# A new order of the calls on all five engines, with the first eight filler matmuls kept and the other 24 taken out

## The chip, the cores and the metric

The kernel runs on one core of one Trainium2 chip. The core has five engines that run side by side, each with its own instruction stream in a fixed order: PE (TensorE, matmuls and transposes), DVE (VectorE), ACT (ScalarE), POOL (GpSimd) and SP (SyncE, here only a queue that issues transfers). They meet at semaphores: an instruction waits until a counter has reached a number, and everything behind it on its engine waits with it. The metric is the device time of one execution in microseconds (us). Three timed executions of the kernel before gave 276.61 us in the median (275.88 to 279.37).

## The reference, cut to what matters

The input is 8 batches of 1024 tokens with 128 features, all float32. One transformer layer is applied to it:

```
q = rope(x @ wq) / sqrt(128);  k = rope(x @ wk) / sqrt(128);  v = x @ wv
p = softmax(causal(q @ k.T))                       # one head, 1024 x 1024 per batch
x1 = layernorm(x + (p @ v) @ wo)
h  = gelu(x1 @ bw1.T + b1)                         # bw = mean|w| * sign(w), 128 -> 512
out = layernorm(x1 + h @ bw2.T + b2)               # 512 -> 128
```

The rotary part turns only the first 64 of the 128 features of q and k; the other 64 are copied.

## The kernel before, in words

A batch (index `c`, 0 to 7; in the code `B - 1` is 7) has 1024 tokens: eight tiles of 128 tokens (index `r` or `t`) in two halves of four (index `h`). Each step of the work is a small function of the engine that does it, and at the end of each engine's block stands a list of calls, written out by hand, some hundreds of lines long. That list is the order. Batches overlap: while the scores of batch `c` are made, the feed-forward part of batch `c - 2` or `c - 3` runs.

The steps of one batch, as they feed one another:

- SP `stripes(c)` (L222): four transfers bring x of batch `c` into `xq`, in pieces of 32 tokens by 32 features. They wait until both halves of the batch before have been turned (`s_xT`), because `xq` is one buffer. For batch 1 the four transfers are not in a call: they stand at L214, third in SP's queue. Their landing counts up `s_xq_in`.
- DVE `x_squares(h, c)` (L1580): transposes `xq` into `xT`. Half 0 waits for all four transfers of its batch. Batch 0 goes another way: `turn_x0` on PE.
- ACT `xT_high`, then POOL `xT_low` (for batch 0 DVE `x0T_low`): split xT in a rounded part and a rest, so that fast matmuls on both parts give float32 accuracy.
- PE `project(h, c)`: q and k of a half. DVE `rotate(h, c)` (L1598): three multiplications with the cosine and sine tables, which ACT's queue loads at the start (L991, L992). ACT `tok_copy`: the features that aren't turned. POOL `rotation_sum` adds the products (for batch 0 DVE `first_rotation_sum`, L1586).
- PE `turn_qk(n, c)`: transposes q (n = 0, 2) and k (n = 1, 3) of a half. ACT `qkT_high` and DVE `qkT_low` (L1617) split them.
- PE `scores(r, c)` into a two-bank tile of PSUM, DVE `row_max`, ACT `exponentials`, DVE `turn_row` (32 by 32 squares). SP `carry(g, c)` (L233): 16 transfers that move the squares between partitions into `probT`; group 0 is rows 0 to 3, group 1 rows 4 to 7. For rows 4 to 7 of batches 0 and 7 PE's `turn_row` with `row_copy` on ACT and DVE takes the place of this.
- PE `weigh_group` or `weigh_row`, ACT `pxT_copy`, PE `project_out`, DVE `residual1`, `statistics1`, POOL `first_factors`, DVE `first_norm`: attention output and first layer norm. `wvo`, the product of wv and wo, is made once by `setup_turn_wv` and `setup_wvo`.
- PE `turn_x1`, ACT `x1T_high`, DVE `x1T_low`, PE `up`, ACT `gelu` and `hidden_high`, POOL `hidden_low`, PE `down`, ACT `y_half`, PE `turn_y`, DVE `residual2`, `statistics2`, POOL `second_factors`, ACT (some POOL) `second_norm`, SP `store`: feed-forward part and second layer norm. Its weights are set up once by ACT `setup_signs`, PE `setup_turn_sgn1` and `setup_turn_sgn2`, ACT `setup_magnitudes` and `setup_weights`.

PSUM has three two-bank tiles (`pairs`) and two single banks (`banks`), handed out in the order of PE's calls. A call that takes one waits until the reader of its last user is done (`wait_freed`, L493).

Two helpers on PE compute nothing: `keep_warm(n)` (L486) and `fill(n)` (L557) multiply a tile of zeros. They are the fillers: `keep_warm` 8 at the very start, then 4, 3 and 6, `fill` 2 in the first batch, 7 and 2 near the end, 32 in all.

Of the kernel before, what the change touches and what calls it, by code (L numbers as in the profile page):

```python
# [16 lines left out]
def attention_ffn_kernel(nc, x, wq, wk, wv, wo, w1, b1, w2, b2, cos_t, sin_t, out):  # L17
# [10 lines left out]
    B, T, D = x.shape  # L28
# [27 lines left out]
    with ctx:  # L56
# [88 lines left out]
        def sems(name, n):  # L145
# [5 lines left out]
            sems("s_qk", NG), sems("s_qkT", 4), sems("s_score", NT), sems("s_px", NT), sems("s_attn", NG))  # L151
# [52 lines left out]
        def _(sp):  # L204
# [28 lines left out]
            def carry(g, c):  # L233
# [4 lines left out]
                if c > 0:  # L238
                    sp.wait_ge(s_px[GROUPS[g][-1]], c)
# [32 lines left out]
            carry(1, 3)  # L272
            stripes(B - 1)
            carry(0, B - 4)
# [3 lines left out]
            carry(0, B - 3)  # L278
            tokens(B - 2)
            store(0)  # L280
            carry(1, B - 3)
            carry(0, B - 2)
            store(1)
# [14 lines left out]
        def _(pool):  # L298
# [96 lines left out]
            xT_low(1, 1)  # L395
            rotation_sum(0, 1)
            rotation_sum(1, 1)
            xT_low(0, 2)
# [3 lines left out]
            xT_low(1, 3)  # L402
            first_factors(0, 0)
            rotation_sum(1, 2)
            rotation_sum(0, 3)
            first_factors(1, 0)
            xT_low(0, B - 4)
            xT_low(1, B - 4)
            rotation_sum(1, 3)
            first_factors(0, 1)  # L410
            first_factors(1, 1)
            rotation_sum(0, B - 4)
            rotation_sum(1, B - 4)
# [3 lines left out]
            xT_low(0, B - 3)  # L417
            hidden_low(3, 0)
            first_factors(0, 2)
            xT_low(1, B - 3)  # L420
            first_factors(1, 2)
            rotation_sum(0, B - 3)
# [5 lines left out]
            first_factors(0, 3)  # L428
            second_factors(0)
            rotation_sum(1, B - 3)  # L430
            first_factors(1, 3)
            xT_low(1, B - 2)
            hidden_low(0, 2)
            rotation_sum(0, B - 2)
            hidden_low(1, 2)
            hidden_low(2, 2)
            hidden_low(3, 2)
            rotation_sum(1, B - 2)
            xT_low(0, B - 1)
# [3 lines left out]
            xT_low(1, B - 1)  # L443
            rotation_sum(0, B - 1)
            hidden_low(0, 3)
            hidden_low(1, 3)
            hidden_low(2, 3)
            hidden_low(3, 3)
            second_factors(2)
            first_factors(0, B - 3)  # L450
            rotation_sum(1, B - 1)
# [3 lines left out]
            hidden_low(2, B - 4)  # L455
            hidden_low(3, B - 4)
            second_factors(3)
# [27 lines left out]
        def _(pe):  # L485
# [71 lines left out]
            def fill(n):  # L557

                wait_freed(*list(pair_of)[-len(pairs)])
                for _ in range(n):  # L560
                    pe.matmul(pairs[len(pair_of) % len(pairs)][:, 0:BANK], warm[:, 0:P], warm[:, :], start=True, stop=True)
# [1569 lines left out]
```

## Time and profile before

| What | Value |
|---|---|
| Timed executions, median of 3 | 276.61 us (275.88 to 279.37) |
| Profiled execution, span from first to last instruction | 274.5 us |
| What lies around the span, against the median | 2.1 us |
| PE busy | 260.9 us, 95% of the span |
| DVE, ACT, POOL busy | 229.6 (84%), 224.7 (82%), 167.2 us (61%) |
| Mean granted TensorE clock | 0.993 of full speed |

The span is that of one profiled execution; no time of its own stands beside it, so it is set against the median. A busy share counts an engine's instructions from start to modelled end, so PE at 95% can still have some slack between the starts of its matmuls. A row of a timeline gives the start, the duration, the engine, the line and what is written and read; in square brackets stands how long the engine was idle before it and who ended that. Waits of SP's queue aren't marked: they show as gaps between its issues.

### The profile page before, as it was taken

What the parts mean: (1) busy time and instruction counts of PE and PEld (TensorE: products, weight loads), DVE (VectorE), ACT (ScalarE), POOL (GpSimd) and SP (SyncE); (2) the same over time, 40 slices, a digit from 0 to 9 for tenths busy, and PEclk for the clock granted to TensorE, in tenths of its full rate; (3) what the DMA queues carried; (4) which work ended last, traced back from release to release, by engine and by line L of the source; (5) the groups of instructions that cost most, each with busy time, mean ns of one, the idle gap of its engine ahead of it and who ended that gap; (6) DMA issues with size and microseconds to landing.
All of it is one profiled execution on the core that took longest, in us unless ns stands there. A gap on an engine that the chain in (4) does not pass through costs nothing.

```text
span 274.5 us, 5184 instructions
## 1 busy us (share of the span) xinstructions
PE 260.9 (95%) x1485; PEld 208.7 (76%) x1487; DVE 229.6 (84%) x638; ACT 224.7 (82%) x398; POOL 167.2 (61%) x258
## 2 busy tenths in 40 slices
PE   7899999999999999999999999999999999999960
PEld 3678989987779588868879688868886878897630
DVE  2799999999999996999979987998689738537984
ACT  3378964565897989996998999898999799999972
POOL 3033132613625698399821998497819887887772
PEclk9999999999999999999999999999999999999997
DMA  7944596479657936833685318825830720200323
GB/s 178 166 61 87 107 145 98 115 163 192 104 132 160 199 94 153 180 47 78 173 187 127 82 39 249 184 71 151 189 73 27 197 55 2 76 2 0 111 90 108
DMA packets 58012, 31.94 MB, mean 116 GB/s; under 512 B 33408, under 2 KB 54400, under 8 KB 57984
## 3 DMA queue, kind: packets, MB, share of 16 engines
q1 hardware_dynamic: 57024, 30.76, 50.4%
q10 hardware_dynamic: 960, 0.85, 1.3%
q8 instruction: 12, 0.20, 0.3%
q14 instruction: 16, 0.13, 0.2%
HBM read 9.18 MB, written 4.19 MB: 49 GB/s over the span
## 4 chain that ended last, share of the span: by engine, by line
PE 81%; DVE 6%; ACT 5%; issue 3%; DMA 2%; ACTq 1%; POOL 0%; POOLq 0%
PE pair L589 18%; PE bank L606 18%; PE bank L632 5%; PE bank L674 4%; PE pair L650 4%; PE pair L651 4%; PE bank L620 4%; PE bank L682 4%; PE bank L683 4%; PE bank L719 2%; DMA sin_sb<-in_sin_dram 2%; PE pair L663 2%; PE pair L665 2%; PE pair L664 2%; PE bank L639 2%
## 5 line engine op out<-in xcount | busy, mean ns | idle before, releaser
L391 POOL TENSOR_TENSOR hid_lo<-hid,hid_hi 128x1024 fp32r<-128x1024 f32 x28 | 66.0, 2386 | 19.7 <-ACT hid_hi L1075 19.7
L1004 ACT ACTIVATE prob<-pair,negmax 128x128 f32<-128x128 f32 (+3 forms) x64 | 47.2, 742 | 14.2 <-DVE negmax L1457 12.5
L606 PE MATMUL bank<-probT,xa 128*128 128x512 f32 (+3 forms) x160 | 54.2, 482 | 0.0
L1457 DVE CUSTOM_DVE_ANT_0 pair<-pair,mask_row 128x128 f32<-128x128 f32 (+3 forms) x64 | 47.9, 759 | 6.1 <-PE pair L589 5.5
L606 PEld LDWEIGHTS bank<-probT,xa 128*128 128x128 f32 x160 | 29.1, 190 | 20.2 <-issue 15.3
L341 POOL TENSOR_TENSOR xT_lo<-xT,xT_hi 128x512 fp32r<-128x512 f32 x14 | 18.0, 1288 | 40.4 <-ACT xT_hi L1034 40.4
L1467 DVE STREAM_TRANSPOSE turned<-prob 128x128 f32<-128x128 f32 (+7 forms) x56 | 39.5, 724 | 0.5 <-ACT prob L1004 0.5
L589 PE MATMUL pair<-qkT_hi 128*128 128x512 f32 (+3 forms) x96 | 36.0, 375 | 0.8 <-DVE qkT_lo L1619 0.3
L1068 ACT ACTIVATE hid<-pair,b_sb,alpha 128x1024 f32<-128x1024 f32 x28 | 32.9, 1209 | 0.1
L589 PE MATMUL pair<-qkT_lo,qkT_hi 128*128 128x512 f32 (+3 forms) x96 | 32.8, 342 | 0.0
L589 PE MATMUL pair<-qkT_hi,qkT_lo 128*128 128x512 f32 (+3 forms) x96 | 32.8, 342 | 0.0
L1075 ACT ACTIVATE hid_hi<-hid 128x1024 fp32r<-128x1024 f32 x28 | 28.6, 1057 | 0.0
L335 POOL TENSOR_TENSOR ln<-ln,minus_half 128x4 f32<-128x4 f32 (+1 forms) x21 | 26.2, 1249 | 1.6
L1102 ACT ACTIVATE res<-res,ln 128x128 f32<-128x128 f32 x52 | 23.1, 496 | 3.6 <-POOL ln L377 3.6
L1056 ACT ACTIVATE qkT_hi<-bank 128x512 fp32r<-128x512 f32 x32 | 18.5, 598 | 7.3 <-PE bank L674 7.2
L1619 DVE TENSOR_TENSOR qkT_lo<-bank,qkT_hi 128x512 fp32r<-128x512 f32 x32 | 21.1, 680 | 3.4 <-ACT qkT_hi L1056 3.4
L349 POOL TENSOR_TENSOR tok<-rot_cos,rot_sin 128x512 f32<-128x512 f32 x14 | 18.0, 1288 | 9.4 <-DVE rot_sin L1614 9.4
L650 PE MATMUL pair<-x1T_hi,sgn1T 128*128 128x512 f32 x56 | 23.4, 418 | 0.3 <-issue 0.3
L682 PE MATMUL bank<-hid_hi,sgn2T 128*128 128x512 f32 x56 | 22.3, 399 | 0.0
L683 PE MATMUL bank<-hid_lo,sgn2T 128*128 128x512 f32 x56 | 22.2, 396 | 0.0
L651 PE MATMUL pair<-x1T_lo,sgn1T 128*128 128x512 f32 x56 | 22.1, 395 | 0.0
L1567 DVE TENSOR_TENSOR res<-bank,x 128x512 f32<-128x512 f32 x16 | 10.9, 687 | 12.5 <-PE bank L719 12.4
(116 smaller groups left out, 649.9 us busy)
## 6 DMA issues: line engine op xcount, KB each, us to landing
probT<-turned SPq DMA_DIRECT2D x96, 116.0 KB, 2.3
probT<-turned SPq DMA_DIRECT2D x128, 52.0 KB, 2.0
xq<-in_L_attn_x_dram SPq DMA_DIRECT2D x28, 128.0 KB, 4.0
xa<-in_L_attn_x_dram SPq DMA_DIRECT2D x7, 512.0 KB, 4.7
out_dram<-res SPq DMA_DIRECT2D x7, 512.0 KB, 3.3
hid<-in_L_ffn_w_dram SPq DMA_DIRECT2D x2, 256.0 KB, 3.2
out_dram<-res SPq DMA_DIRECT2D x2, 256.0 KB, 2.3
xa<-in_L_attn_x_dram SPq DMA_DIRECT2D x1, 256.0 KB, 3.6
```

The costliest lines, as they stand in the source:

```text
L391: pool.tensor_tensor(hid_lo[:, j, :], hid[:, j, :], hid_hi[:, j, :].bitcast(F32), ALU.subtract).then_inc(s_hid_lo[j], 1)
L589: ins = pe.matmul(dst[:, lo:hi], qp[:, 0, me], kp[:, 1, lo - first:hi - first], start=n == 0, stop=n == 2)
L606: ins = pe.matmul(bank_of["px", g, c][:, 0:n * P], xa[c % 2][:, j, :], probT[g][:, :, TG * j:TG * j + n, :].rearrange("p n m i -> p m n i" ...
L650: pe.matmul(dst[:, half(h)], sgn1T[:, j, :], x1T_hi[:, half(h)], start=True, stop=False)
L651: ins = pe.matmul(dst[:, half(h)], sgn1T[:, j, :], x1T_lo[:, half(h)], start=False, stop=True)
L682: pe.matmul(dst[:, :], sgn2T[:, j, :], hid_hi[:, j, half(h)], start=j == 0, stop=False)
L683: ins = pe.matmul(dst[:, :], sgn2T[:, j, :], hid_lo[:, j, half(h)], start=False, stop=j == NF - 1)
L1004: act.activation(prob[r % 3][:, 0:(r + 1) * P], pair_of["score", r, c][:, slice(*columns(r))], ACT.Exp, scale=-1.0, bias=negmax[:, r:r + 1 ...
L1068: act.activation(hid[:, j, :], pair_of["up", j, c][:, :], ACT.Gelu, bias=b1_sb[:, j:j + 1], scale=alpha1[:, j:j + 1]).then_inc(s_gelu[j], 1)
L1075: act.activation(hid_hi[:, j, :], hid[:, j, :], ACT.Copy).then_inc(s_hid_hi[j], 1)
L1457: dve.tensor_tensor_reduce(mine, mine, mask_row[:, T - (r + 1) * P:T], -1.0, -MASKED, ALU.add, ALU.min, negmax[:, r:r + 1]).then_inc(s_max ...
L1467: dve.transpose(turned[g][:, :, squares(r, 0, r), :].rearrange("p k m j -> p m k j"), prob[r % 3][:, 0:(r + 1) * P].rearrange("p (m k j) - ...
```

## The change

It keeps every call but the fillers, and puts the lists of all five engines in another order. Of the fillers only `keep_warm(8)` stays; `fill` and its definition go. The semaphore `s_px` has one counter for each group of rows in place of one for each row; the waits on it mean what they meant. The diff has some 1,600 lines; these are the parts that matter at the start, in SP's queue and at the end.

```diff
@@ SP
             stripes(3)
+            stripes(B - 4)
             tokens(1)
-            stripes(B - 4)
             carry(0, 1)
             carry(1, 1)
+            stripes(B - 3)
             tokens(2)
-            stripes(B - 3)
...
@@ PE, start
             turn_x0(0)
             turn_x0(1)
-            keep_warm(4)
             project(0, 0)
             project(1, 0)
-            keep_warm(3)
             turn_qk(0, 0)
             turn_qk(1, 0)
-            keep_warm(6)
             setup_turn_wv()
             scores(0, 0)
+            setup_wvo()
             scores(1, 0)
-            fill(2)
-            turn_qk(2, 0)
             scores(2, 0)
             scores(3, 0)
-            setup_wvo()
+            turn_qk(2, 0)
+            turn_qk(3, 0)
             project(0, 1)
-            turn_qk(3, 0)
             project(1, 1)
+            scores(4, 0)
             setup_turn_sgn1()
             setup_turn_sgn2()
-            scores(4, 0)
...
             project(0, 3)
             project_out(1, 0)
+            weigh_group(0, 0, 3, 1)
+            turn_qk(2, 2)
             scores(0, 2)
             scores(1, 2)
-            weigh_group(0, 0, 3, 1)
-            turn_qk(2, 2)
...
@@ PE, end
             down(1, B - 2)
             turn_x1(1, B - 1)
-            fill(7)
             turn_y(0, B - 2)
             turn_y(1, B - 2)
-            fill(2)
             up_half(1, 0, B - 1)
...
@@ ACT, start
             xT_high(0, 0)
             xT_high(1, 0)
+            xT_high(0, 1)
             tok_copy(0, 0)
             qkT_high(0, 0)
             qkT_high(1, 0)
             tok_copy(1, 0)
-            xT_high(0, 1)
+            exponentials(0, 0)
+            xT_high(1, 1)
+            exponentials(1, 0)
+            exponentials(2, 0)
+            qkT_high(2, 0)
+            exponentials(3, 0)
+            qkT_high(3, 0)
             setup_signs()
-            exponentials(0, 0)
-            exponentials(1, 0)
-            xT_high(1, 1)
-            exponentials(2, 0)
-            exponentials(3, 0)
-            qkT_high(2, 0)
-            qkT_high(3, 0)
             setup_magnitudes()
             tok_copy(0, 1)
+            xT_high(0, 2)
             tok_copy(1, 1)
...
@@ DVE, start
             setup_wqk()
             x0T_low(0)
             x0T_low(1)
+            x_squares(0, 1)
+            x_squares(1, 1)
             rotate(0, 0)
             first_rotation_sum(0)
             rotate(1, 0)
-            x_squares(0, 1)
             qkT_low(0, 0)
             qkT_low(1, 0)
+            setup_wvT()
             first_rotation_sum(1)
-            setup_wvT()
             row_max(0, 0)
+            x_squares(0, 2)
             row_max(1, 0)
-            x_squares(1, 1)
+            row_max(2, 0)
             turn_row(0, 0)
-            row_max(2, 0)
+            setup_wvo()
             row_max(3, 0)
-            setup_wvo()
...
             row_max(4, 0)
+            x_squares(1, 2)
             row_max(5, 0)
...
             row_max(1, 1)
-            qkT_low(2, 1)
-            qkT_low(3, 1)
-            rotate(0, 2)
-            row_max(2, 1)
-            turn_row(0, 1)
-            turn_row(1, 1)
             x_squares(0, 3)
             x_squares(1, 3)
+            qkT_low(3, 1)
+            row_max(2, 1)
             row_max(3, 1)
+            turn_row(1, 1)
```

From batch 1 on the lists are shuffled throughout, mostly by one to three places on PE and by up to some ten on DVE and ACT; no call changes its engine, its size or its waits.

## Rows read from the trace of the kernel before

**Rows 1.** Stretches: us, busy (instructions) of PE, PEld, DVE, ACT, POOL, granted clock, DMA, GB/s.
```profile
27.26:32.32 5.06, 4.96 (x43) 4.44 (x42) 4.86 (x11) 5.06 (x13) 0.76 (x1) 1.00 0.31 78
32.40:246.40 214.00, 213.04 (x1216) 173.32 (x1215) 184.07 (x511) 183.07 (x310) 140.83 (x209) 1.00 0.54 122
...
267.10:270.70 3.60, 0.00 (x0) 0.00 (x0) 2.69 (x13) 0.88 (x2) 2.22 (x4) 1.00 0.34 103
270.90:274.40 3.50, 0.00 (x0) 0.00 (x0) 0.53 (x2) 0.80 (x2) 0.00 (x0) 0.50 0.48 149
```
**Rows 2.** PE's waits: who it waited for, us in total, times, longest.
```profile
PE bank L719 <- ACT yT L1093: 1.2, 2, 1.0
```
**Rows 3.** Chain of waits, first 40 us: start us, us, what.
```profile
2.21 6.63 DMA sin_sb<-in_sin_dram
8.87 0.69 DVE rot_cos L1611
...
12.21 0.62 DVE xT L1584
...
13.93 1.78 DVE tok L1589
...
22.57 0.61 ACT tok L1041
```
**Rows 4.** The four transfers of x of batch 1: durations, starts; issue to landing.
```profile
L214 SPq DMA_DIRECT2D xq<-in_L_attn_x_dram x4: 443/1484/3146, 1.8 to 6.1; - x4
...
DMA to landing us min/median/max: 5.4/7.1/7.9
```
**Rows 5.** Timelines of DVE, POOL and ACT: start us, us, what [idle before <- ended by].
```profile
10.26 0.69 DVE L1589 TENSOR_TENSOR tok<-rot_cos,rot_sin 128x512 f32<-128x512 f32 x1
...
13.87 1.29 POOL L341 TENSOR_TENSOR xT_lo<-xT,xT_hi 128x512 fp32r<-128x512 f32 x1 [10.23 <-ACT xT_hi L1034]
...
13.66 0.64 ACT L1009 ACTIVATE hid<-hid 128x512 f32<-128x512 f32 x1
...
28.78 1.12 ACT L1004 ACTIVATE prob<-pair,negmax 128x1024 f32<-128x1024 f32 x1
```
**Rows 6.** Timeline of PE in the first 16 us.
```profile
9.62 0.82 PE L489 MATMUL pair<-warm 128*128 128x512 bf16 x3
11.00 1.09 PE L674 MATMUL bank<-ident,tok 128*128 128x128 f32 x8 [0.56 <-DVE tok L1589]
...
14.15 0.30 PE L589 MATMUL pair<-qkT_hi 128*128 128x128 f32 x1 [0.29 <-DVE qkT_lo L1619]
```
**Rows 7.** Timeline of PE from 27.26 us: first and last of five rows, all transposes.
```profile
27.26 0.60 PE L674 MATMUL bank<-ident,tok 128*128 128x128 f32 x4
...
31.96 0.60 PE L674 MATMUL bank<-ident,tok 128*128 128x128 f32 x4
```
**Rows 8.** Timeline of SP's queue: start us, us, transfers issued.
```profile
31.11 2.70 SPq L226 DMA_DIRECT2D xq<-in_L_attn_x_dram  x4
...
38.52 2.32 SPq L226 DMA_DIRECT2D xq<-in_L_attn_x_dram  x4
40.94 22.25 SPq L242 DMA_DIRECT2D probT<-turned  x32
```
**Rows 9.** The page, issues of transfers: KB each, median us from issue to landing.
```profile
probT<-turned SPq DMA_DIRECT2D x128, 52.0 KB, 2.0
xq<-in_L_attn_x_dram SPq DMA_DIRECT2D x28, 128.0 KB, 4.0
```
**Rows 10.** Timelines of PE and ACT: one row at 54 us, then near the end.
```profile
54.58 2.32 PE L606 MATMUL bank<-probT,xa 128*128 128x512 f32 x8
...
254.89 1.46 PE L561 MATMUL pair<-warm 128*128 128x512 bf16 x6
...
257.30 0.59 PE L561 MATMUL pair<-warm 128*128 128x512 bf16 x2
...
255.47 0.78 ACT L1093 ACTIVATE yT<-bank,b_sb,alpha 128x512 f32<-128x512 f32 x1
```

More of the change, by code:

```diff
@@ L609, in weigh_group @@
                 if last == rows[-1]:
-                    ins.then_inc(s_px[last], 1)
+                    ins.then_inc(s_px[g], 1)
             def weigh_row(r, c):
@@ L755, in _ @@
             turn_row(7, 0)
-            turn_qk(3, 1)
+            project(0, 2)
             scores(0, 1)
             scores(1, 1)
-            project(0, 2)
+            weigh_group(0, 0, 3, 0)
+            turn_qk(3, 1)
             scores(2, 1)
-            weigh_group(0, 0, 3, 0)
             scores(3, 1)
+            project_out(0, 0)
             scores(4, 1)
+            turn_qk(0, 2)
             scores(5, 1)
-            project_out(0, 0)
             scores(6, 1)
-            turn_qk(0, 2)
             scores(7, 1)
@@ L839, in _ @@
             scores(4, B - 4)
+            turn_y(1, 0)
             project_out(0, 3)
-            weigh_group(1, 0, 3, 3)
             scores(5, B - 4)
             scores(6, B - 4)
+            weigh_group(1, 0, 3, 3)
             weigh_group(1, 4, 7, 3)
@@ L901, in _ @@
             scores(7, B - 2)
+            weigh_group(1, 0, 3, B - 3)
+            weigh_group(1, 4, 7, B - 3)
             turn_x1(1, B - 4)
-            weigh_group(1, 0, 3, B - 3)
+            project(1, B - 1)
             turn_qk(0, B - 1)
-            weigh_group(1, 4, 7, B - 3)
+            turn_qk(1, B - 1)
             up(0, B - 4)
             up(1, B - 4)
-            turn_qk(1, B - 1)
-            project(1, B - 1)
             project_out(1, B - 3)
@@ L915, in _ @@
             up(3, B - 4)
+            turn_y(1, 3)
+            turn_qk(2, B - 1)
             scores(0, B - 1)
-            turn_y(1, 3)
+            scores(1, B - 1)
             weigh_group(0, 0, 3, B - 2)
-            scores(1, B - 1)
-            turn_qk(2, B - 1)
+            turn_qk(3, B - 1)
             scores(2, B - 1)
-            turn_qk(3, B - 1)
             scores(3, B - 1)
@@ L961, in _ @@
             weigh_row(7, B - 1)
+            up(3, B - 2)
+            turn_y(1, B - 3)
             turn_x1(0, B - 1)
@@ L1149, in _ @@
             qkT_high(2, 1)
[L1150 removed]
             exponentials(0, 1)
[L1152 to L1153 removed]
             tok_copy(0, 2)
             pxT_copy(0, 0)
+            qkT_high(3, 1)
+            exponentials(1, 1)
+            xT_high(0, 3)
             exponentials(2, 1)
@@ L1171, in _ @@
             qkT_high(2, 2)
+            exponentials(0, 2)
             qkT_high(3, 2)
@@ L1208, in _ @@
             xT_high(1, B - 3)
-            x1T_high(1, 1)
-            exponentials(5, 3)
             exponentials(6, 3)
             pxT_copy(1, 2)
+            x1T_high(1, 1)
+            tok_copy(1, B - 4)
             qkT_high(0, B - 4)
@@ L1734, in _ @@
             first_norm(7, 0)
-            statistics1(0, 1)
+            residual1(0, 1)
+            residual1(1, 1)
+            residual1(2, 1)
+            residual1(3, 1)
+            x1T_low(0, 0)
+            turn_row(3, 2)
             turn_row(4, 2)
+            x1T_low(1, 0)
+            row_max(6, 2)
+            reciprocals(0, 2)
             row_max(7, 2)
-            x1T_low(1, 0)
+            rotate(1, 3)
+            qkT_low(0, 3)
             turn_row(5, 2)
             turn_row(6, 2)
-            reciprocals(0, 2)
-            statistics1(1, 1)
-            statistics1(2, 1)
-            statistics1(3, 1)
             turn_row(7, 2)
@@ L1850, in _ @@
             x1T_low(1, 2)
+            rotate(0, B - 2)
             residual1(4, 3)
@@ L1913, in _ @@
             residual1(7, B - 4)
-            statistics2(1, 1)
+            rotate(0, B - 1)
+            qkT_low(2, B - 2)
             statistics1(4, B - 4)
```

736 lines of the change are left out of this document (359 added, 377 removed).

## The prediction

> **What bounds the kernel now.** I read the stretches first. From 32.4 to 246.4 us PE is busy for 213.04 of 214.00 us at the full granted clock [rows 1]: in the middle PE is the bound, and a new order can win at most the 1.0 us of idle time there (a little more if slack hides between the starts of its matmuls). The middle is nearly eight tenths of the span, so what the order can change for the better lies mostly before and behind it. Whatever PE loses at the start it doesn't get back, since it has no idle time in which to catch up.
>
> Next, the chain of waits of the first 40 us. The start isn't PE's. The sine table lands after 2.21 + 6.63 = 8.84 us, DVE begins the first rotation at 8.87, and from there the chain runs along DVE almost without a break to 22.57 [rows 3]; only then does it pass to PE. So a microsecond that DVE loses before 22.57 is one that the whole kernel loses. Two pieces on this chain matter below: the transpose of x of batch 1 (12.21, 0.62 us) and the second rotation sum (13.93, 1.78 us).
>
> Then the queue. The four transfers of x of batch 1 were issued between 1.8 and 6.1 us, and none landed in under 5.4 us [rows 4]. The last one therefore landed at 6.1 + 5.4 = 11.5 us or later. In the kernel before nobody notices, because the transpose that needs them starts only at 12.2.
>
> **The change part by part.** *The first transposes.* In the new list of DVE x_squares(0, 1) and x_squares(1, 1) stand ahead of rotate(0, 0). The first waits for all four transfers, and DVE takes its calls strictly in turn. So DVE stands still until 11.5, transposes twice (2 x 0.62 [rows 3]) and starts the first rotation at about 12.8 instead of 8.87: **+3.9 us**. Queued behind are the rotation sum, both copies of ACT, and turn_qk on PE; everything of batch 0 waits for those. Nothing else in the change touches these transfers: the queues of SP and ACT keep their first calls as they are.
>
> Part of it comes back. The transpose at 12.21 is no longer between rotation and scores: **-0.6** (x_squares(0, 2) comes in later, in the place of the second transpose). The second rotation sum took 1.78 us beside a subtraction of POOL (13.87, 1.29 us), the first one 0.69 with POOL idle [rows 3, 5]. In the new order that subtraction follows the transpose at about 13 and is over before either sum: **-1.1**.
>
> Part is added. ACT's two sign activations ran before at 13.66, when ACT had nothing else to do; a pair of them takes about 1.1 us [rows 5]. They and xT_high(0, 2), another 0.6, now stand ahead of tok_copy(1, 1). I follow ACT from the shifted rotation on: most of it is hidden behind DVE's work for the same rows, some 0.5 us shows, and 0.2 us more where DVE waits for ACT's first copy of q: **+0.7**. So the exponentials of row 7, batch 0, at 28.78 before [rows 5], move by 3.9 - 0.6 - 1.1 + 0.7 = **+2.9**, and the transposes of rows 6 and 7 on PE with them. Bounds of this: +2.2 if ACT's added work is hidden whole, +4.3 if POOL's subtraction still collides and the waits stand (3.9 - 0.6 + 0.7, and 0.3).
>
> *A second landing of the same kind.* x_squares(0, 3) now stands right behind row_max(1, 1), ahead of qkT_low(3, 1) and row_max(2, 1). Its transfers are issued in 2.7 us from 31.11 before [rows 8], now some 3.4 us later because carry(0, 0) is; with 4.0 us to land [rows 9] they are there at about 40.5. I count DVE there at about 38. Behind it wait scores(4, 1) and the exponentials of rows 2 and 3; PE has other calls for most of that time. **+0.4**, bounds 0 and the whole 2.5.
>
> *The fillers at the start.* keep_warm(4), (3), (6) and fill(2) all stand in front of work that waits for something else (turn_qk for the rotation sum, scores for qkT_low [rows 6]); taking them out gives **0**. What they cover is the clock. With them gone PE is idle from about 9.9 until turn_qk(0, 0), which moves from 11.00 to about 15.0: 5.1 us. At the end of the trace the granted clock was still 1.00 at 270.7, 3.6 us after PE's last instruction, and 0.50 (1.2 GHz) from 270.9 [rows 1]. 5.1 is longer than 3.6, so I expect the clock to fall before PE starts again. The calls that then run at half speed on the chain: turn_qk(0, 0) takes 0.44 more, scores(0, 0) 0.36 more (it takes 0.36 from 14.15 to the next call), turn_qk(2, 0) and (3, 0) 0.4 more each: **+1.6**. Bounds: 0, if the clock stays, and +3, if both project(_, 1) (2 x 1.5 us) run at half speed too and DVE has no slack for it.
>
> The Trainium skill has a rule that bears on this stretch (TensorE: Matmul & The Clock Gate, section Part 4: PE-mode transpose): transposes on PE don't count as busy for the clock. This case's trace doesn't show it: from 27.26 to 32.32 PE did nothing but 43 transposes and the clock stayed at 1.00 [rows 1, 7], whereas 3.6 us without any instruction ended in its fall. By the rule the two turn_qk at 15 us would not help the clock back up; that is a rival below.
>
> *The fillers near the end.* fill(7) runs until 254.89 + 1.46 = 256.35, but turn_y waits for ACT's yT, which ends at 255.47 + 0.78 = 256.25 [rows 10]: 0. fill(2) takes 0.59 at most [rows 10] of which half is pipeline: **-0.3**. The gaps there stay under 2 us, so the clock should hold.
>
> *The rest.* On PE most calls move by one to three places. That the middle has 1.0 us to win and no bound below for what a bad neighbour can cost makes me take **0**, with -1 and +3 as ends. s_px is a renaming: 0.
>
> **Sum.** 2.9 + 0.4 + 1.6 - 0.3 = +4.6 us on the span of 274.5: 279.1. Around the span lie 2.1 us against the median of 276.61 (276.61 - 274.5), so 281.2 us, or 1.7% over it. A measurement tells about 2% from no change here: 271.1 and 282.1 us are the borders.
>
> **The rivals.**
>
> *A, the sum above:* 281.2; with its own terms between 279.5 and 283.
>
> *B, the clock holds.* The 5.1 us gap might straddle what the clock looks at, or turn_qk may come in time. 281.2 - 1.6 = 279.6. For it: one fall in the whole trace is thin evidence. Against it: the gap is longer than the one after which it fell.
>
> *C, SP's queue becomes the bound: slower.* carry(0, 1) starts at 40.94, right behind stripes(4), which waited until 38.52 for x_squares(1, 3); two carries take 22.25 us to issue, one half of that [rows 8]. So the last transfer of carry(0, 1) is issued near 52.1 and lands 2.0 us later [rows 9], at 54.1, while weigh_group(0, 0, 3, 1) takes it at 54.58 [rows 10]: 0.5 us to spare. In the new order tokens(1) (0.6) moves in between, x_squares(1, 3) waits for the later landing above, and weigh_group(0, 0, 3, 1) comes two calls (0.8) earlier. If the queue shifts by more than PE does, PE waits in this batch and, as the queue issues without a break for batch after batch, in the next ones. It decides from about half a microsecond of extra shift; once there, the price is the queue's shift of 3.5 on top: 284.7.
>
> *D, the start is won back: no slower.* If the clock holds, the second landing is hidden, and the new order removes the 1.0 us of idle time in the middle [rows 1] and the 1.2 us for yT at the end [rows 2]: 274.5 + 2.9 - 0.3 - 1.0 - 1.2 + 2.1 = 277.0. It needs everything to go well at once in the rows that a new order can reach.
>
> *E, transposes don't count for the clock (the rule of the Trainium skill above).* It falls and comes back only in the course of project(0, 1) and (1, 1): half of the 3.0 us more that those two take at half speed shows, +1.5 over A: 282.7. Rows 7 speak against it.
>
> **How the numbers follow.** A 0.45, B 0.24, C 0.17, D 0.10, E 0.04. The predicted time is A's, 281.2 us. D at its low side and the upper half of C stay out of the range: 277.0 to 284.7. A lies within 2% in three cases of four, so slower by over 2%: 0.11 (A) + 0.17 (C) + 0.03 (E) = 0.31. Faster by over 2% would need 5.5 us, more than all idle time that rows 1 and 2 leave: 0.03. Within 2%: 0.66.
>
> **What would show it.** Right: in DVE's timeline an idle time of some 4 us ahead of the first transpose, ended by the transfer of xq; rot_cos first at about 12.8; PE idle from 9.9 to about 15; a granted clock of 0.5 somewhere between 13 and 25 us; the middle still PE's, shifted as a whole by 4 to 5 us. Wrong: rot_cos near 9 (then the landing isn't as late as I read it), a clock of 1.00 throughout (B), new waits of PE for probT between 50 and 120 us (C), or a chain of waits that leaves PE in the middle.

## The result: 301.06 us, and where the time went

The kernel after takes 301.06 us (median; 300.6 to 301.33) against 276.55 of the kernel before (four executions of each): a ratio of 1.0877, 95% interval [1.0822, 1.0932]. The profiled execution has a span of 299.2 us and took 301.02. I had predicted 281.2 with 284.7 as the upper end; the loss is 24.5 us, five times the 4.6 of my sum.

PE's waits of after, the five largest of the whole span (us in total, times, longest us; in before the largest was the 1.2 us of [rows 2]):

```profile
PE bank L633 <- DVE x L1487: 9.3, 5, 3.8
PE bank L668 <- DVE tok L1577: 4.4, 1, 4.4
PE bank L633 <- DVE res L1473: 2.8, 1, 2.8
PE bank L713 <- ACT yT L1081: 2.7, 2, 1.6
PE bank L668 <- DVE x1T_lo L1548: 2.6, 2, 1.6
```

One row of these was predicted: the 4.4 us for tok is the start. The largest wasn't. Line 633 is turn_x1, which transposes the first norm's output, and L1487 is first_norm on VectorE (line 1499 of before). In the middle, where PE had 1.0 us of idle time in 214 [rows 1], PE now waits for VectorE. The same in stretches of after, for PE alone (stretch, us, PE busy, granted clock, DMA share, GB/s):

```profile
13.50:23.70 10.20, 8.11 (x32) 0.50 0.40 53
23.80:90.00 66.20, 66.03 (x431) 1.00 0.60 125
90.00:231.00 141.00, 129.22 (x682) 1.00 0.50 115
231.95:235.37 3.42, 3.42 (x12) 0.50 1.02 275
235.40:252.40 17.00, 12.88 (x67) 1.00 0.15 38
252.43:255.85 3.42, 3.42 (x16) 0.50 0.02 5
```

Up to 90 us the middle is full, as before. From 90 to 231 us PE is idle for 11.8 us, and the clock falls to 0.50 (1.2 GHz) in two more stretches of 3.42 us. Each begins about 1 us after a stop of PE, the one of 2.76 us (it ends at 230.96) and the other of 3.76 (at 251.38). A step that both kernels have shows the same without any grouping; the start of scores(7, c) on PE, after minus before, in us:

```
batch c      0     1     2     3     4     5     6      7    last call of PE
shift     +4.9  +4.8  +4.3  +6.3  +8.1  +9.8  +14.0  +17.3   +24.7
```

So 4.9 us are lost in batch 0, nothing in the next two, 13.0 in the five batches behind them and another 7.4 behind the last scores, 20.4 in all.

What VectorE does there is in the view of one line (duration ns min/median/max, first and last start, forms). first_norm of after:

```profile
L1487 DVE TENSOR_SCALAR x<-res,ln x64: 306/341/2427, 61.3 to 278.2; 128x128 f32<-128x128 f32 x64
L1473 DVE SCALAR_TENSOR_TENSOR res<-bank,rinv,xa x64: 305/340/351, 46.2 to 274.7; 128x128 f32<-128x128 f32 x64
```

The same line in before:

```profile
L1499 DVE TENSOR_SCALAR x<-res,ln x64: 306/342/436, 56.2 to 253.1; 128x128 f32<-128x128 f32 x64
```

The median has not changed; 19 of the 64 are over 0.4 us now, and the group's busy time is 42.8 us instead of 18.7. Its neighbour residual1 (L1473), of the same size, is as fast as ever. What a long one stands beside is seen in the timeline of after between 94 and 104 us, VectorE first (start, us, operation; "x2" are two in a row):

```profile
94.14 0.34 DVE L1487 TENSOR_SCALAR x<-res,ln 128x128 f32<-128x128 f32 x1
94.40 1.12 DVE L1473 SCALAR_TENSOR_TENSOR res<-bank,rinv,xa 128x128 f32<-128x128 f32 x4
95.44 0.68 DVE L1599 TENSOR_TENSOR rot_cos<-pair,cos_sb 128x512 f32<-128x512 f32 x1
96.69 1.48 DVE L1487 TENSOR_SCALAR x<-res,ln 128x128 f32<-128x128 f32 x1
98.10 1.09 DVE L1445 CUSTOM_DVE_ANT_0 pair<-pair,mask_row 128x896 f32<-128x896 f32 x1
99.11 3.68 DVE L1487 TENSOR_SCALAR x<-res,ln 128x128 f32<-128x128 f32 x2
102.71 1.43 DVE L1455 STREAM_TRANSPOSE turned<-prob 128x512 f32<-128x512 f32 x2
```

and POOL and PE in the same stretch:

```profile
95.73 6.98 POOL L391 TENSOR_TENSOR hid_lo<-hid,hid_hi 128x1024 fp32r<-128x1024 f32 x3 [2.91 <-ACT hid_hi L1063]
102.85 0.66 PE L633 MATMUL bank<-ident,x 128*128 128x128 f32 x4 [2.00 <-DVE x L1487]
```

first_norm(4, 1) at 94.14 takes 0.34 us with POOL idle. From 95.73 POOL runs three hidden_low in a row, each about 2.3 us. The next first_norm takes 1.48 and ends at 98.17, just when the first hidden_low is over; the two at 99.11 end at 102.79, just behind the third. In between row_max (98.10) runs at its own speed beside the second hidden_low, and the transposes behind 102.71 do beside POOL's next instruction. PE waits 2.00 us for the last first_norm. In before all four calls stood ahead of rotate(1, 4) and row_max(6, 3). The last two of them, and the first hidden_low, in before:

```profile
89.69 0.60 DVE L1499 TENSOR_SCALAR x<-res,ln 128x128 f32<-128x128 f32 x2
93.12 7.04 POOL L391 TENSOR_TENSOR hid_lo<-hid,hid_hi 128x1024 fp32r<-128x1024 f32 x3
```

They were through at 90.3, and POOL began at 93.1. The new order puts the last three of the four behind rotate(1, 4), two of them behind row_max(6, 3) too, and so into POOL's stretch. Such meetings occur in batches 2 to 7 as well. Of the 19 long first_norm, 16 end just behind a hidden_low and 3 just behind POOL's xT_low, a subtraction of 128x512 that takes 1.29 us.

Not every POOL instruction has this effect. Two first_norm of batch 3 beside a small one of POOL, in after:

```profile
151.49 0.59 DVE L1487 TENSOR_SCALAR x<-res,ln 128x128 f32<-128x128 f32 x2
151.45 1.04 POOL L335 TENSOR_TENSOR ln<-ln,minus_half 128x4 f32<-128x4 f32 x1
```

They took their usual time and were done 0.4 us ahead of POOL. All 20 first_norm that began beside one of POOL's small instructions (128x4 to 128x16) took less than 0.4 us.

The start went as predicted. VectorE and PE of after:

```profile
11.21 1.30 DVE L1572 STREAM_TRANSPOSE xT<-xq 128x512 f32<-128x512 f32 x2 [3.34 <-DMA xq<-in_L_attn_x_dram]
12.44 0.65 DVE L1599 TENSOR_TENSOR rot_cos<-pair,cos_sb 128x512 f32<-128x512 f32 x1
14.54 1.97 PE L668 MATMUL bank<-ident,tok 128*128 128x128 f32 x8 [4.41 <-DVE tok L1577]
```

Against [rows 3] the rotation begins at 12.44 instead of 8.87, behind two transposes that wait for xq.

The chain of waits of after passes to VectorE accordingly, by engine and by line (page):

```profile
PE 63%; DVE 24%; issue 5%; DMA 2%; ACT 2%; POOL 1%; SPq 1%; ACTq 0%; POOLq 0%; DVEq 0%
PE pair L583 13%; DVE x L1487 9%; PE bank L600 7%; PE bank L668 5%; PE bank L676 4%; PE bank L677 4%; PE bank L626 4%; PE pair L644 4%; PE pair L645 4%; PE bank L614 4%; DVE pair L1445 4%; DVE turned L1455 3%; PE pair L685 2%; DVE stat L1564 2%; DMA xq<-in_L_attn_x_dram 2%
```

### The profile page after: what moved, and what is told of

Its sections match the earlier page's. It is cut to its first block, busy times and chain, and to the rows that moved or that the text cites. A ratio compares the mean times of both kernels' runs of the same rounds, so it can differ in the third digit from the quotient of the medians.

```text
span 299.2 us, 5138 instructions
## 1 busy us (share of the span) xinstructions
PE 264.5 (88%) x1463; PEld 213.4 (71%) x1463; DVE 253.2 (85%) x638; ACT 225.4 (75%) x398; POOL 167.9 (56%) x258
## 4 chain that ended last, share of the span: by engine, by line
PE 63%; DVE 24%; issue 5%; DMA 2%; ACT 2%; POOL 1%; SPq 1%; ACTq 0%; POOLq 0%; DVEq 0%
PE pair L583 13%; DVE x L1487 9%; PE bank L600 7%; PE bank L668 5%; PE bank L676 4%; PE bank L677 4%; PE bank L626 4%; PE pair L644 4%; PE pair L645 4%; PE bank L614 4%; DVE pair L1445 4%; DVE turned L1455 3%; PE pair L685 2%; DVE stat L1564 2%; DMA xq<-in_L_attn_x_dram 2%
## 5 line engine op out<-in xcount | busy, mean ns | idle before, releaser
L391 POOL TENSOR_TENSOR hid_lo<-hid,hid_hi 128x1024 fp32r<-128x1024 f32 x28 | 65.9, 2376 | 22.4 <-ACT hid_hi L1063 22.2
L992 ACT ACTIVATE prob<-pair,negmax 128x128 f32<-128x128 f32 (+3 forms) x64 | 47.3, 741 | 25.6 <-DVE negmax L1445 20.4
L600 PE MATMUL bank<-probT,xa 128*128 128x512 f32 (+3 forms) x160 | 53.6, 483 | 0.6 <-DMA probT<-turned 0.3
L600 PEld LDWEIGHTS bank<-probT,xa 128*128 128x128 f32 x160 | 29.5, 190 | 24.2 <-issue 18.7
L1487 DVE TENSOR_SCALAR x<-res,ln 128x128 f32<-128x128 f32 x64 | 42.8, 713 | 1.5 <-POOL ln L369 0.9
L1455 DVE STREAM_TRANSPOSE turned<-prob 128x128 f32<-128x128 f32 (+7 forms) x56 | 38.7, 715 | 1.6 <-ACT prob L992 1.5
L583 PE MATMUL pair<-qkT_lo,qkT_hi 128*128 128x512 f32 (+3 forms) x96 | 34.0, 354 | 0.0
L583 PE MATMUL pair<-qkT_hi,qkT_lo 128*128 128x512 f32 (+3 forms) x96 | 34.0, 354 | 0.0
L668 PE MATMUL bank<-ident,tok 128*128 128x128 f32 x128 | 20.0, 292 | 7.3 <-DVE tok L1577 4.4
L323 POOL TENSOR_TENSOR ln<-stat 128x4 f32<-128x4 f32 (+1 forms) x21 | 4.4, 210 | 37.3 <-DVE stat L1478 28.9
L1090 ACT ACTIVATE res<-res,ln 128x128 f32<-128x128 f32 x52 | 22.3, 492 | 3.8 <-POOL ln L377 3.6
L668 PEld LDWEIGHTS bank<-ident,tok 128*128 128x128 f32 x128 | 16.1, 152 | 9.7 <-issue 4.7
```

Source lines behind the costliest of these rows:

```text
L391: pool.tensor_tensor(hid_lo[:, j, :], hid[:, j, :], hid_hi[:, j, :].bitcast(F32), ALU.subtract).then_inc(s_hid_lo[j], 1)
L583: ins = pe.matmul(dst[:, lo:hi], qp[:, 0, me], kp[:, 1, lo - first:hi - first], start=n == 0, stop=n == 2)
L600: ins = pe.matmul(bank_of["px", g, c][:, 0:n * P], xa[c % 2][:, j, :], probT[g][:, :, TG * j:TG * j + n, :].rearrange("p n m i -> p m n i" ...
L668: ins = pe.transpose(dst[:, t * P:(t + 1) * P], tok[:, TG * (n // 2) + t, (n % 2) * D:(n % 2 + 1) * D], ident[:, :])
L992: act.activation(prob[r % 3][:, 0:(r + 1) * P], pair_of["score", r, c][:, slice(*columns(r))], ACT.Exp, scale=-1.0, bias=negmax[:, r:r + 1 ...
L1455: dve.transpose(turned[g][:, :, squares(r, 0, r), :].rearrange("p k m j -> p m k j"), prob[r % 3][:, 0:(r + 1) * P].rearrange("p (m k j) - ...
```

## The experiments

Where an edit adds lines to the kernel, the lines behind it move by two or three in the rows: first_norm is then L1489, L1490 or L1501 and hidden_low L393.

Theory L: a first_norm that is due while a POOL instruction runs stands still until that instruction ends, and this is where the middle goes. (By the rows above, "a POOL instruction" has to be read as one of its large subtractions.) Theory O: the order's other waits hold the middle, and the long first_norm is a by-product. Theory P, for one run: it is POOL's length, hid_lo being late, that costs.

### Taking POOL's long instruction away, with a control

```diff
 def hidden_low(j, c):
+    if c == 0: pool.memset(hid_lo[:, j, P:T].bitcast(F32), 0.0)
-    pool.tensor_tensor(hid_lo[:, j, :], hid[:, j, :], hid_hi[:, j, :].bitcast(F32), ...)
+    pool.tensor_tensor(hid_lo[:, j, 0:P], hid[:, j, 0:P], hid_hi[:, j, 0:P].bitcast(F32), ...)
```

The rest of hid_lo is set to zero once, so seven eighths of this correction are left out.

> The changed kernel with POOL's hidden_low cut from 1024 to 128 columns (the other columns of hid_lo are set to zero once, so the low part of the hidden layer is left out there). Theory L (a DVE first_norm that starts while a POOL instruction is running stands still until that one ends): the 19 first_norm that took up to 2.43 us in the changed kernel fall to about 0.34, DVE's total for them from 42.8 to some 22 us, PE's waits for them (9.3 us) go, and the time falls by about 19 us to 280 to 284 us; what stays is the start's 4.8 us. Theory O (the place of first_norm in DVE's list is what PE waits for, whatever POOL does): first_norm may get shorter but PE's waits ahead of turn_x1 stay, 296 to 301 us.

> The control: the same cut of POOL's hidden_low in the kernel before. There only one first_norm of 64 was longer than 0.4 us, so by theory L, and by theory O, nothing is won: 274 to 278 us. If this one falls by 5 us or more as well, POOL's work itself was a bound, and the cut in the changed kernel proves nothing of the meeting of DVE and POOL.

Measured: 280.21 us in the order of after (1.0125 times before, [1.0076, 1.0173]) and 276.63 in the order of before (0.9999, [0.9979, 1.002]). The groups of a_small_lo (busy us, mean ns, idle before):

```profile
L1489 DVE TENSOR_SCALAR x<-res,ln 128x128 f32<-128x128 f32 x64 | 20.6, 367 | 1.8 <-POOL ln L369 1.2 <-POOL ln L335 0.6
L393 POOL TENSOR_TENSOR hid_lo<-hid,hid_hi 128x128 fp32r<-128x128 f32 x28 | 13.0, 466 | 33.7 <-ACT hid_hi L1065 33.6
```

and first_norm of the control:

```profile
L1501 DVE TENSOR_SCALAR x<-res,ln 128x128 f32<-128x128 f32 x64 | 18.6, 338 | 0.6 <-POOL ln L369 0.3
```

The order of before doesn't care how long hidden_low is; the order of after gets 20.9 us back, and PE's wait for x is gone. What is left over the control, 3.6 us, is the start: PE's scores(7, c) is 5.2 us late in batch 0 and between 4.3 and 5.1 in all others, and its last call 3.9. Part of the 20.9 us comes by way of the clock: without the stops it stays at 1.00 from 23.3 us to the end of PE's work, and the two stretches of 3.42 us at half speed are gone, by estimate 1.7 us each.

### Making POOL wait instead

```diff
 def hidden_low(j, c):
+    if j == 0:
+        pool.wait_ge(s_x1[1] if c < 5 else s_x1[0], c + 2)
     pool.wait_ge(s_hid_hi[j], c + 1)
```

> The changed kernel, whole computation, with one wait more on POOL: hidden_low(0, c) starts only when the first_norm of the half that met it (second half of batch c+1, for c = 5 and 6 first half of batch c+2) is done. No call changes its place. Theory L: the long first_norm go (all but a few under 0.4 us), POOL's hidden_low move back by 2 to 4 us, which its idle time of 44% takes; 281 to 288 us. Theory O: a wait more can only cost, 300 to 306 us.

For c = 5 and 6 the edit waits for the first half of batch c + 1, not c + 2 as written there. Measured: 305.37 us (1.1043, [1.0993, 1.1093]): a miss for L's number, and inside O's 300 to 306. The groups of a_yield, and then four of PE's waits:

```profile
L393 POOL TENSOR_TENSOR hid_lo<-hid,hid_hi 128x1024 fp32r<-128x1024 f32 x28 | 65.9, 2375 | 51.0 <-DVE x L1489 46.6 <-ACT hid_hi L1065 4.4
L1489 DVE TENSOR_SCALAR x<-res,ln 128x128 f32<-128x128 f32 x64 | 25.3, 441 | 5.0 <-POOL ln L335 4.2 <-POOL ln L369 0.9
```

```profile
PE bank L678 <- POOL hid_lo L393: 6.6, 5, 2.0
PE bank L715 <- ACT yT L1083: 5.1, 3, 2.4
PE bank L635 <- DVE x L1489: 5.0, 1, 5.0
PE bank L602 <- DVE qkT_lo L1609: 2.5, 1, 2.5
```

first_norm did get short (25.3 us), and PE's project(0, 6), at 133.5 us, comes 5.0 earlier than in after. But POOL now stands idle for 46.6 us until first_norm is through, with all that follows in its list late too: PE waits 6.6 us for POOL's hid_lo, a wait that after does not have, and scores(5, 5), at 159.2 us, is already 1.8 later than in after. The clock is at 0.50 for 17.1 us behind 150 us, against 6.8 in after. So the run adds a wait of its own and can't decide between L and O by its time. I had left out the price of that wait: POOL's list had no room for it.

### Cutting hidden_low into four

```diff
-    pool.tensor_tensor(hid_lo[:, j, :], hid[:, j, :], hid_hi[:, j, :].bitcast(F32),
-                       ALU.subtract).then_inc(s_hid_lo[j], 1)
+    for q in range(4):
+        part = slice(q * T // 4, (q + 1) * T // 4)
+        ins = pool.tensor_tensor(hid_lo[:, j, part], hid[:, j, part], hid_hi[:, j, part].bitcast(F32),
+                                 ALU.subtract)
+    ins.then_inc(s_hid_lo[j], 1)
```

> The kernel after, where each hidden_low (POOL, 128x1024) is issued as four instructions of 256 columns; the result is the same and its total POOL time grows: from the 128x128 form's 0.46 us and the 128x1024 form's 2.37 us a piece is some 0.73 us, so four are 2.93, and 28 of them cost POOL 15 us more. Theory L (VectorE's first_norm stands still while a POOL instruction runs, and a stop ends with the POOL instruction): the longest first_norm falls from 2.43 us to about 1.1, the excess of all 64 over their 0.34 from 24 us to 8 to 14, and the time from 301 to 287 to 293. Theory P (it is POOL's own length, or hid_lo being late, that costs, and cutting hidden_low short removed that): 301 to 312. Theory O (the order's other waits): 299 to 303.

Measured: 286.95 us (1.0358, [1.0303, 1.0413]), 14.1 less than after, with all work done. The groups of a_split4:

```profile
L393 POOL TENSOR_TENSOR hid_lo<-hid,hid_hi 128x256 fp32r<-128x256 f32 x112 | 78.1, 731 | 17.0 <-ACT hid_hi L1066 16.9
L1490 DVE TENSOR_SCALAR x<-res,ln 128x128 f32<-128x128 f32 x64 | 29.3, 502 | 1.5 <-POOL ln L369 0.9 <-POOL ln L335 0.6
```

POOL works 12 us longer and the kernel is 14 us faster, so P falls. The longest first_norm is 892 ns now, the length of a piece (731) plus a part of its own: of the 27 over 0.4 us, 26 end just behind a piece and one behind xT_low. O had 299 to 303; L had 287 to 293, and the time lies at its lower end.

### Only the order, the instructions untouched

```diff
 first_norm(4, 1)
+first_norm(5, 1); first_norm(6, 1); first_norm(7, 1)    # from behind rotate(1, 4), row_max(6, 3)
 ...
+residual2(1, 0); first_norm(4..7, 2)                    # ahead of turn_row(2, 4)
 ...
 first_norm(4, 3)
+first_norm(5..7, 3)                                     # from behind turn_row(3, 5)
 ...
 first_norm(4, 5)
+first_norm(5..7, 5)                                     # from behind turn_row(3, 7)
```

> The kernel after with thirteen calls of VectorE's list put earlier and nothing else: first_norm(5..7,1), (5..7,3) and (5..7,5) directly behind first_norm(4,.) of their batch, and residual2(1,0) with first_norm(4..7,2) ahead of turn_row(2,4), so that these groups are done when POOL's next hidden_low begins. In the trace of after these 13 calls carry 15.3 of the 24 us by which first_norm is longer than 0.34 each. Theory L (it is only that first_norm meets hidden_low): first_norm's excess falls to 8 to 11 us, and the time from 301 to 285 to 291. Theory O (the new order's other waits hold the middle; the same instructions in a slightly other order change nothing): 298 to 303.

Measured: 288.11 us (1.0417, [1.0356, 1.0478]), 12.9 less than after: thirteen first_norm and one residual2 put earlier in one engine's list give back half of the loss. VectorE of a_early where the rows above were taken:

```profile
94.45 1.10 DVE L1487 TENSOR_SCALAR x<-res,ln 128x128 f32<-128x128 f32 x4
95.47 1.12 DVE L1473 SCALAR_TENSOR_TENSOR res<-bank,rinv,xa 128x128 f32<-128x128 f32 x4
```

and POOL:

```profile
96.04 7.05 POOL L391 TENSOR_TENSOR hid_lo<-hid,hid_hi 128x1024 fp32r<-128x1024 f32 x3 [2.91 <-ACT hid_hi L1063]
```

Four first_norm in 1.10 us, over before POOL begins at 96.04. The group's busy time falls from 42.8 to 28.0; eight long ones are left, six of them in batches 4, 6 and 7, which I had not touched. The time is in L's range; O, with 298 to 303, fails here too.

### Another instruction for first_norm

```diff
-ins = dve.tensor_scalar(x1[c % 2][:, t, :], res1[:, t, :], ln1[:, 2, t:t + 1], ln1[:, 7, t:t + 1],
-                        ALU.subtract, ALU.mult)
+ins = dve.scalar_tensor_tensor(x1[c % 2][:, t, :], res1[:, t, :], ln1[:, 2, t:t + 1],
+                               ln1[:, 7, t:t + 1].broadcast_to([P, D]), ALU.subtract, ALU.mult)
```

> The kernel after with first_norm as scalar_tensor_tensor (its rstd column as a broadcast second tensor, so two tensor inputs in SBUF) instead of tensor_scalar (one). In the traces the only other VectorE instruction that grew beside POOL's was the rotation sum of before, a tensor_tensor whose inputs both lie in SBUF (1.78 us for 0.69), while scalar_tensor_tensor with one input in PSUM (residual1, 32 of them under POOL) stayed at 0.35. If both forms with all operands in SBUF stand still: first_norm's maximum stays near 2.4 us and the time is 300 to 303. If tensor_scalar alone does: first_norm at 0.30 to 0.45 everywhere and 279 to 283.

Measured: 303.3 us (1.0948, [1.0901, 1.0994]), 0.3 above the range for "both forms stand still" and far from the other. The views of two lines of a_stt:

```profile
L1487 DVE SCALAR_TENSOR_TENSOR x<-res,ln x64: 311/348/2450, 60.8 to 278.7; 128x128 f32<-128x128 f32 x64
L1473 DVE SCALAR_TENSOR_TENSOR res<-bank,rinv,xa x64: 303/344/356, 45.7 to 275.2; 128x128 f32<-128x128 f32 x64
```

One operation, one size, two lines: with both tensors in SBUF it stands still like tensor_scalar (2.45 us), with one of them in PSUM it doesn't (0.36 at most, with 30 of the 64 beside POOL, 10 of these beside a hidden_low). So the operation's name isn't what counts; where its tensors lie is part of it.

### The start: the waits for xq

a_start moves x_squares(0, 1) and (1, 1) behind rotate(1, 0), and xT_high(0, 1) behind tok_copy(1, 0). a_start2 goes further back towards the order of before:

```diff
 x0T_low(1)
-x_squares(0, 1)
-x_squares(1, 1)
 rotate(0, 0)
 first_rotation_sum(0)
 rotate(1, 0)
+x_squares(0, 1)
 ...
 row_max(0, 0)
-x_squares(0, 2)
+x_squares(1, 1)
 ...
 qkT_low(3, 0)
+x_squares(0, 2)
```

> The changed kernel with x_squares(0, 1) and x_squares(1, 1) put back behind rotate(1, 0) on DVE, and ACT's xT_high(0, 1) behind tok_copy(1, 0). Theory S (DVE's stand for the landing of xq, and the clock's fall in PE's gap that follows from it, are the start's 4.8 us): first rotation back at about 8.9, PE's gap under 2 us, granted clock 1.00 from 5 to 30 us, all calls of batch 0 earlier by 3.5 to 4.8 us, 296 to 298 us. If the start is lost elsewhere (ACT's signs, the order of scores): less than 2 us won, 299 to 301 us.

> The kernel after, with the start's steps put as before had them: x_squares(0,1) behind rotate(1,0), x_squares(1,1) behind row_max(0,0), x_squares(0,2) behind qkT_low(3,0), xT_high(0,1) behind tok_copy(1,0). a_start moved only the first two and the last, and VectorE then waited 3.06 us for xq at x_squares(0,2), ahead of row maxima and wvo that PE waited 2.0 us for. If the start's shift (4.9 us on PE's steps of batch 0) comes from these waits for xq alone: no wait of VectorE for xq over 0.5 us in the first 30 us, PE's scores(7,0) back at 26.0 to 27.5 instead of 30.75, and 296.5 to 298.5. If PE's own order of calls holds the start: as a_start, 299.5 to 301.

Two places in a_start2 are not those of before, as the expectation has it: before has x_squares(1, 1) behind row_max(1, 0), and x_squares(0, 2) only behind row_max(7, 0) and qkT_low(0, 1).

Measured: a_start 300.14 us (1.0848, [1.0807, 1.0888]), which is 0.9 less than after and a miss for theory S; a_start2 298.83 (1.0796, [1.0715, 1.0876]). The four executions of a_start2 lie between 296.96 and 300.62, so its time alone doesn't show a gain; the trace does. In a_start the rotation is back at 8.65 us, but x_squares(0, 2) now waits for its transfers in front of row maxima and of wvo. Its row on VectorE, and PE's wait behind it:

```profile
18.80 0.71 DVE L1572 STREAM_TRANSPOSE xT<-xq 128x512 f32<-128x512 f32 x1 [3.06 <-DMA xq<-in_L_attn_x_dram]
```

```profile
PE bank L668 <- DVE wvo L1437: 2.0, 1, 2.0
```

Pulling two transposes out of the way only moved the wait to the next. With all three moved back (a_start2), PE's scores(7, 0) is 1.8 us late instead of 4.9, and the last call 21.4 instead of 24.7. Time and call are both a little above what I expected (298.83 against 298.5, scores(7, 0) at 27.65 against 27.5). x_squares(0, 2), still earlier in the list than in before, waits 1.2 us for its transfers, and PE waits 1.6 us for ScalarE's second copy of q (tok), with ScalarE's list still in the new order. The clock, too, still falls. PE in a_start2, busy and granted clock:

```profile
14.48:17.89 3.41, 3.34 (x12) 0.50 0.21 33
```

PE had stopped there for 0.81 us at 9.8 and for 1.46 at 11.7. How the 1.8 us divide among the three was not tried.

### The start: the clock

```diff
+keep_warm(4)
 project(0, 0)
 ...
+keep_warm(20)
 turn_qk(0, 0)
 ...
+keep_warm(6)
 setup_turn_wv()
```

> The kernel after with filler matmuls put back: 4 ahead of project(0,0), 20 ahead of turn_qk(0,0), 6 ahead of setup_turn_wv. The clock term of the prediction: PE is idle from 10.1 to 14.5 us, the granted clock falls to 0.50 at 13.5 and is 1.00 again at 23.7, and that was put at 1.6 us. If the idle stretch brings the low clock and the low clock costs that: granted clock 1.00 from 10 to 24 us and 299 to 300 us. If the clock costs nothing there, because PE waits for VectorE anyway: 300.7 to 301.5.

Measured: 298.97 us (1.0784, [1.0738, 1.083]), 2.1 less than after. The stretch of a_fill in place of the first of PE's stretches in after (there 8.11 busy at 0.50):

```profile
13.50:23.70 10.20, 9.70 (x67) 1.00 0.38 53
```

The granted clock stays at 1.00 (2.4 GHz), and scores(7, 0) is 1.9 us late instead of 4.9. The idle time of 4.4 us did bring the low clock, and the low clock cost 2 to 3 us.

### Both together

a_best is a_early with the edits of a_start2 and a_fill; a_close has the short hidden_low of a_small_lo with the same two edits.

> a_early with the start of a_start2 (x_squares and xT_high as before) and the fillers of a_fill. If the meetings and the start are separate and add up: 12 to 15 us from the first, 4 to 5 from the start: 281 to 286. If the start's gain is eaten by new meetings (a start that is earlier by 4.9 us shifts VectorE against POOL nowhere, since both follow PE): the same. If the order has other costs: over 288.

> The kernel after with hidden_low cut to 128 of its 1024 columns (the other columns of hid_lo are zeroed once, so seven eighths of that correction are left out), the start of a_start2 and the fillers of a_fill. It closes the sum: a_small_lo has 280.2 where the control, before with the same cut, has 276.6, and PE's shift of 5 us in batch 0 is the only one left. If two causes make up all of the loss: 275.5 to 277.5. If a third one is left in the middle: 278 to 281.

Measured: a_best 286.61 us (1.0373, [1.0328, 1.0417]) and a_close 279.0 (1.0094, [1.0051, 1.0136]), both above what I expected if the parts add up, and a_close in the range that I gave to a third cause in the middle (278 to 281). The parts don't add up, but the trace puts the reason at the start. PE of a_close:

```profile
9.98 4.49 PE L491 MATMUL pair<-warm 128*128 128x512 bf16 x19
14.31 1.04 PE L670 MATMUL bank<-ident,tok 128*128 128x128 f32 x8
```

The twenty fillers of a_fill were sized for the 4.4 us that PE was idle in after. With the rotation early again, its first sum is done at 11.4 us and turn_qk could go (in a_start it starts at 10.79), but the fillers hold PE until 14.3. scores(7, 0) is 4.0 us late instead of 1.8 without them, and PE waits 2.2 us for ScalarE's tok on the way there (1.6 in a_start2). That the other 2.4 us of a_close over the control go this way is argued from these rows; the run without the fillers wasn't made. The shift in a_close is never larger behind batch 0 than in it (2.3 to 3.9, against 4.0), so there is no third cause in the middle.

### The same stop in the kernel before

```diff
 first_rotation_sum(1)
+x_squares(0, 1)        # VectorE, from behind rotate(1, 0)
 ...
+xT_high(0, 1)          # ScalarE, from behind tok_copy(1, 0)
 exponentials(0, 0)
```

> The kernel before with x_squares(0,1) moved behind first_rotation_sum(1), and ScalarE's xT_high(0,1) ahead of exponentials(0,0), so that POOL's first xT_low no longer runs when VectorE does its second rotation sum (1.78 us for it in before, 0.69 for the first). Theory L: the sum takes 0.69 and, as the chain of waits of before runs through it, the time falls by up to 1.1: 275.3 to 276.2. If the sum's length has another cause: 1.78 again and 276.4 to 277.5.

Measured: 275.46 us against 276.95 of before beside it: 0.9952, [0.9923, 0.998], so half a per cent faster than before and the fastest of all kernels here. The two rotation sums of b_sum:

```profile
L1589 DVE TENSOR_TENSOR tok<-rot_cos,rot_sin x2: 681/686/691, 10.3 to 13.6; 128x512 f32<-128x512 f32 x2
```

The second had taken 1.78 us in before, beside POOL's subtraction [rows 3, 5]. With POOL's instruction later (15.68), it takes 0.68. The sum is done 1.4 us earlier, 1.1 by its length and 0.3 because the transposition now stands behind it, and PE's last call comes 1.0 earlier.

### The runs side by side

first_norm's busy time and the kernel's, in us:

```
kernel      first_norm busy   time
before           18.7        276.55
a_small_lo       20.6        280.21
a_early          28.0        288.11
a_split4         29.3        286.95
after            42.8        301.06
a_stt            44.0        303.3
a_yield          25.3        305.37   (POOL waits instead)
```

From after down to a_small_lo, 22.2 us less of first_norm are 20.9 us less of the kernel: nearly as much, with the clock's part in it. a_yield is the exception: there the stop was handed to POOL, and the kernel lost the time all the same.

## Why the prediction was wrong

**The step that failed is "The rest".** I took 0 for the calls that move in the middle, with +3 as the upper end. It measured 20.9 us: VectorE's first_norm, due beside POOL's subtractions, comes late, and PE waits for it. "No bound below for what a bad neighbour can cost" was right as a sentence, and then I put a bound all the same, without working out one. The rows to do so were there. [rows 3, 5] show a VectorE instruction at 1.78 us beside a POOL instruction and at 0.69 without, and I used that only for the 1.1 us that the change gives back there. Had I asked which other VectorE calls have all their tensors in SBUF, first_norm would have been on the list, 64 of them (beside transposes and statistics, which the runs show unharmed), and the largest POOL work to be met is 28 hidden_low of 2.38 us. In after it came to nineteen meetings, sixteen with hidden_low and three with xT_low, of 1.3 us each. Whether they meet can't be read off the list alone. But the list shows three first_norm moving from ahead of rotate(1, 4) to behind it, two of them behind row_max(6, 3), and in the trace of before that row_max runs at 94.2, beside hidden_low.

The Trainium skill has the rule (SBUF — State Buffer, section Who interferes with whom): VectorE and GpSimd share one pair of SBUF ports as an exclusive lock, VectorE takes it for a tensor_scalar in a two-port mode and, against a GpSimd instruction that reads SBUF, for an instruction with two inputs in SBUF, and the second to issue "fully blocks" until the first has finished. The large subtractions agree with it: 2.43 us for first_norm beside a hidden_low of 2.38, 0.89 beside a piece of 0.73, 2.45 for the form with two inputs in SBUF, 0.36 for the one with an input in PSUM. POOL's tensor_tensor of 128x4 doesn't: first_norm took 0.34 us beside it with 1.0 us of it left. The profile's spans of POOL are rough, so why is open; and that first_norm runs in a two-port mode no run here shows. I had not weighed it against the change, and it is the rule that speaks against it.

**The first transposes: right.** The idle time ahead of the transpose was 3.34 us, the rotation came at 12.44 (I had 12.8), and PE's calls of batch 0 were 4.9 late, where my terms for them come to 4.5 (2.9 + 1.6). That the sum is so near is luck in part: with the clock held (a_fill), 1.9 of the 4.9 are left, so the waits' own part was nearer 2 than 2.9, and the clock's larger than its term.

**The clock: right in kind, too small.** PE was idle for 4.4 us, the granted clock fell to 0.50 at 13.5 us and was back at 23.7. I had 1.6; the fillers bring 2.1 in time and 3.0 in the shift of batch 0. Rival B falls with it. I had let the fall hang on a gap longer than 3.6 us; in after it also came behind a stop of 2.76 us, and in a_start2 with none over 1.46. That transposes don't help the clock (rival E) isn't needed for anything that is seen.

**The second landing: not there.** The transposes for batch 3 begin at 41.15 us, directly behind a row maximum, with no wait for xq. I had VectorE there at 38 and the transfers at 40.5. The +0.4 should have been 0, because VectorE itself came late enough.

**The fillers near the end** made no difference that can be told from the rest; no run puts them back alone.

**Rival C, SP's queue:** PE's wait for probT was 0.3 us in all. **Rival D:** nothing was won back. I named a chain of waits that leaves PE in the middle as what would prove me wrong, and so it was: VectorE has 24% of the chain in after, 9% of it first_norm alone. But the mechanism of the loss stood among none of the rivals: A, B, D and E were mainly about the edges of the span, because PE was full in the middle, and C was about SP's queue. A full engine can't be made fuller, but it can be made to wait, and then the middle has the longest stretch to lose time in.

Without most of the meetings, and with seven eighths of that correction left out, the kernel takes 280.21 us (a_small_lo), 1.0 below the prediction. Since the control gains nothing by the same cut, the rest of the sum was near, though not term by term.

## What to carry to other kernels

Ahead of a reordering, list the VectorE instructions that a POOL instruction holds up in the trace you have (a maximum far over the median, ended with the other engine's instruction), and then see which of them the new lists bring together; the price of a meeting is what is left of the other engine's instruction, here 1.3 us on average and 2.1 at most. A wait on one engine costs what is queued behind it, and cutting the long instruction into pieces was cheaper here than a wait for the right moment (286.95 against 305.37 us). Fillers are sized for one idle time: with an earlier start the same fillers can stand in its way, as a_close suggests.

## What the runs showed of the hardware

- A tensor_scalar of VectorE on float32 with its input and output in SBUF (128x128, 0.34 us) took up to 2.43 us when a POOL subtraction from SBUF to SBUF of 128x1024 or 128x512 was running, and ended 0.08 to 0.09 us behind that instruction. Beside POOL's instructions of 128x4 to 128x16 it kept under 0.4 us (20 cases). POOL's hidden_low was never lengthened: 2.34 to 2.44 us for all 28 in after.
- scalar_tensor_tensor does the same with both tensors in SBUF (2.45 us) and not with one in PSUM (0.36). In after stream transposes and statistics, which read SBUF, kept their times beside POOL (128x512: 0.71 us at most with and without; BATCH_NORM_STATS2 at most 0.30).
- A stop of PE of 4.41 us at 10.1 us was followed by a granted clock of 0.50 from 13.5 to 23.7. Two more stretches at 0.50 came behind stops of 2.76 and 3.76 us and lasted 3.42 us each, with PE busy through all of both. In a_start2 a stretch at 0.50 (14.48 to 17.89) came behind stops of 0.81 and 1.46 us.
